# A transformer layer on one core: the score scale moved into queries and keys, maxima stored negated, and the weight maxima in another order

## What is computed

```python
q = (norm(x) @ Wqa @ Wqb)            # 16 heads x (64 plain + 64 rotary)
c_kv, k_pe = split(norm(x) @ Wkva)   # 64 latent + 64 rotary, shared by all heads
q_pe, k_pe = rope(q_pe), rope(k_pe)
scores = q_full @ k_full.T * 128 ** -0.5, causal
probs = softmax(scores)
attn = probs @ v ; x = x + attn @ Wo
x = x + top-2-of-16 experts(norm(x)) + shared expert(norm(x))
```

## Time and profile before

| | us |
|---|---|
| time before, median of 3 runs (1613.17 to 1618.74) | 1617.57 |
| the profiled execution, its own time | 1630.28 |
| its span, first to last instruction | 1627.2 |

### The profile page before, as it was taken

One profiled execution on the slowest core, in us unless ns is written; L12 is line 12 of the kernel. 1 busy time (PEld: TensorE's weight loads), 2 busy tenths in 40 slices (PEclk: granted clock), 3 DMA queues, 4 the chain that ended last, 5 costly groups with the idle time before them and its releaser, 6 DMA issues.

```text
span 1627.2 us, 45245 instructions
## 1 busy us (share of the span) xinstructions
PE 1500.0 (92%) x16430; PEld 1089.0 (67%) x16431; DVE 1290.8 (79%) x3107; ACT 1030.5 (63%) x2344; POOL 989.1 (61%) x1596
## 2 busy tenths in 40 slices
PE   9878999999889999998899999988999999889990
PEld 3355777777667777776667777766677777667870
DVE  2587888888878889888788888888787888766676
ACT  1366666666667666666566666665766666557770
POOL 3257774536288754656888777677886755264440
PEclk6799999999999999999999999999999999999995
DMA  6255753321363333203643322135543210347518
GB/s 189 37 120 134 165 83 63 65 58 35 63 123 70 75 65 70 58 17 72 110 92 70 70 61 54 29 73 95 104 67 63 58 34 16 103 123 242 162 56 314
DMA packets 331031, 144.69 MB, mean 89 GB/s; under 512 B 278498, under 2 KB 321541, under 8 KB 330824
## 3 DMA queue, kind: packets, MB, share of 16 engines
q1 hardware_dynamic: 305744, 105.67, 32.3%
q10 hardware_dynamic: 18168, 19.41, 4.0%
q0 software_dynamic: 6912, 16.83, 3.1%
HBM read 47.04 MB, written 29.53 MB: 47 GB/s over the span
## 4 chain that ended last, share of the span: by engine, by line
PE 64%; DVE 16%; ACT 5%; DMA 4%; issue 4%; SPq 1%; POOL 1%; ACTq 0%; DVEq 0%; POOLq 0%
PE of_ps L698 26%; PE s_ps L698 23%; PE t_ps L872 13%; DVE pT L1668 5%; DMA qT<-work 2%; DVE smax L1639 2%; DVE smax L1621 2%; ACT pT L1065 1%; ACT probs L1199 1%; PE of_ps L980 1%; PE t_ps L966 1%; ACT work L1065 1%; DVE weights L1878 1%; DVE o_sb L1502 1%; DVE smax L1643 1%
## 5 line engine op out<-in xcount | busy, mean ns | idle before, releaser
L1668 DVE TENSOR_TENSOR pT<-t_ps,pT 128x512 f16<-128x512 f32 (+3 forms) x688 | 409.7, 598 | 121.3 <-ACT pT L1065 118.4
L1065 ACT CAST pT<-t_ps 128x512 f16<-128x512 f32 (+3 forms) x688 | 354.6, 515 | 230.2 <-PE t_ps L872 229.0
L698 PE MATMUL s_ps<-kT,qT 128*128 128x512 f16 (+3 forms) x2112 | 474.9, 337 | 4.4 <-DMA qT<-work 3.7
L872 PE MATMUL t_ps<-id,probs 128*128 128x128 f32 x2304 | 381.0, 280 | 27.1 <-DVE pT L1668 15.9
L872 PEld LDWEIGHTS t_ps<-id,probs 128*128 128x128 f32 x2304 | 256.7, 142 | 123.1 <-issue 73.7
L1194 ACT ACTIVATE probs<-s_ps,nmax,fac 128x640 f32<-128x640 f32 (+3 forms) x256 | 269.1, 1051 | 0.2
L698 PEld LDWEIGHTS of_ps<-ckv,pT 128*128 128x128 f16 x6912 | 241.0, 98 | 41.8 <-DVE o_sb L1502 10.1
L698 PE MATMUL of_ps<-ckv,pT 128*128 128x64 f16 x6912 | 257.8, 193 | 7.7 <-DVE o_sb L1502 7.4
L698 PEld LDWEIGHTS s_ps<-kT,qT 128*128 128x128 f16 x2112 | 203.7, 98 | 71.6 <-DMA qT<-work 4.4
L698 PE MATMUL of_ps<-weights,xT 128*128 128x512 f16 (+1 forms) x936 | 197.9, 348 | 17.6 <-ACT work L1065 5.5
L1948 POOL TENSOR_TENSOR os_<-o_sb,os_ 128x512 f16<-128x512 f32 x60 | 70.1, 1169 | 153.3 <-ACT os_ L1065 151.4
(11 more groups left out here) (238 smaller groups left out, 2476.8 us busy)
## 6 DMA issues: line engine op xcount, KB each, us to landing
wgu_sb<-wgu ACTq DMA_DIRECT2D x8, 704.0 KB, 4.7
work<-lists SPq DMA_DIRECT2D x40, 128.5 KB, 2.3
qT<-lists SPq DMA_DIRECT2D x40, 128.5 KB, 2.8
x_sb<-x SPq DMA_DIRECT2D x32, 128.0 KB, 2.5
x<-x SPq DMA_DIRECT2D x32, 128.0 KB, 2.5
dense<-den SPq DMA_DIRECT2D x32, 128.0 KB
weights<-dense ACTq DMA_DIRECT2D x1, 4096.0 KB, 21.4
qT<-y_exp SPq DMA_DIRECT2D x16, 256.0 KB, 6.8
```

Source lines behind the costliest of these rows:

```text
L698: return pe_.matmul(o, a, b, start=start, stop=stop)
L872: last = pe_.transpose(t_ps[:, h, c * P:(c + 1) * P], probs[:, u % 2, g * L + j * P:g * L + (j + 1) * P], id32[:, :])
L1065: return act.copy(o, i)
L1668: dve.tensor_tensor(pT[:, u % 2, 1, h, 0:w], t_ps[:, h, 0:w], pT[:, u % 2, 0, h, 0:w], ALU.subtract).then_inc(s.lo_p, 1)
```

## The change

Four things are changed together.

1. `f_att` is split into two factors. `f_root` is about one over its square root, from the float's bits; keys are scaled by `f_k = 1 / f_root`, queries by `f_q = f_att * f_root`, as they are copied out of PSUM, and the output projection's factor takes `f_root` to undo the keys' part in `ckv`. Scores then come out of TensorE finished, and the exponentials need no scale.
2. Maxima are stored negated by the reduction itself, straight into `nmax`. The second instruction is gone, but for tile 7, where the smaller of the two negated halves is still to be found.
3. `SPLIT_MAX` picks halves for tiles 0 to 3 and 7; tile 6 goes by whole units now.
4. In `first_weights` the maxima of the query weights' blocks come as the blocks do, the other weights' maxima and the two `means` in between; `scales` is raised a first time before the new factors are made.

```diff
-SPLIT_MAX = [g > 1 or i >= 6 for i, g in enumerate(GROUP)]
+SPLIT_MAX = [g > 1 or i == 7 for i, g in enumerate(GROUP)]
...
+            def scaled(o, i, factor):
+                return act.activation(o, i, ACT.Copy, scale=factor)
...
-                copy(pe_of(n)[:, H, :], bank[:, C:2 * C])
-                copy(ks_sb[:, n % KS, 0, 0:C], bank[:, 0:C]).then_inc(s.hi_q, 1)
+                scaled(pe_of(n)[:, H, :], bank[:, C:2 * C], f_k)
+                scaled(ks_sb[:, n % KS, 0, 0:C], bank[:, 0:C], f_k).then_inc(s.hi_q, 1)
...
-                        act.activation(probs[:, par, 0:L], s_flat[:, 1024 * par:1024 * par + L], ACT.Exp, bias=nmax[:, par, 0:1],
-                                       scale=f_att, accum_out=ssum[:, t % 2, u:u + 1]).then_inc(s.exp_done, 2)
+                        act.activation(probs[:, par, 0:L], s_flat[:, 1024 * par:1024 * par + L], ACT.Exp, bias=nmax[:, par, 0:1],
+                                       accum_out=ssum[:, t % 2, u:u + 1]).then_inc(s.exp_done, 2)
...
+                dve.sem_inc(s.scales, 1)
                 link(dve.tensor_scalar(f_att, wamp[:, A_Q:A_Q + 1], wamp[:, A_KV:A_KV + 1], HD ** -0.5, ALU.mult, ALU.mult))
-                dve.tensor_scalar(f_natt, f_att, -1.0, None, ALU.mult)
+                link(dve.tensor_scalar(f_root.bitcast(I32), f_att.bitcast(I32), -0.5, SEED_K, ALU.mult, ALU.add))
+                dve.reciprocal(f_k, f_root)
+                link(dve.tensor_tensor(f_q, f_att, f_root, ALU.mult))
                 dve.sem_inc(s.scales, 1)
...
-                dve.tensor_tensor(ks_sb[:, n % KS, 1, 0:C], bank_of("lat", n)[:, 0:C], ks_sb[:, n % KS, 0, 0:C],
-                                  ALU.subtract).then_inc(released("lat", n)[0], 1)
+                dve.scalar_tensor_tensor(ks_sb[:, n % KS, 1, 0:C], bank_of("lat", n)[:, 0:C], f_k, ks_sb[:, n % KS, 0, 0:C],
+                                         ALU.mult, ALU.subtract).then_inc(released("lat", n)[0], 1)
...
-                dve.tensor_reduce(smax[:, par, 0:G], view, AX_X, ALU.max).then_inc(s.maxs, 1)
-                dve.wait_ge(s.maxs, g_ + 1)
...
+                most = dve.tensor_reduce(nmax[:, par, 0:G], view, AX_X, ALU.max, negate=True)
+                if not shifted(i, u):
+                    most.then_inc(s.max_ready, 1)
                     return
-                dve.tensor_scalar(nmax[:, par, 0:G], smax[:, par, 0:G], f_natt, None, ALU.mult).then_inc(s.max_ready, 1)
...
-                    last = dve.tensor_scalar(nmax[:, par, 0:1], smax[:, par, 0:1], smax[:, par, 1:2], f_natt, ALU.max, ALU.mult)
+                dve.tensor_tensor(nmax[:, par, 0:1], smax[:, par, 0:1], smax[:, par, 1:2], ALU.min).then_inc(s.max_ready, 1)
```

More of the change, by code:

```diff
@@ L128 @@
 SEED = 1597463007.0
+SEED_K = SEED - 3 * 2.0 ** 23
 A_Q, A_KV, A_O, A_SG, A_SD, A_R, A_GU, A_D = range(8)
@@ L1199, in exps @@
                     last = act.activation(probs[:, par, g * L:(g + 1) * L], s_flat[:, base:base + L],
-                                          ACT.Exp, bias=nmax[:, par, g:g + 1], scale=f_att,
+                                          ACT.Exp, bias=nmax[:, par, g:g + 1],
                                           accum_out=ssum[:, t % 2, u * G + g:u * G + g + 1])
@@ L1251, in section @@
                 side(t, units(t), 0)
+            act.wait_ge(s.scales, 2)
             latent_copies(0)
```

69 lines of the change are left out of this document (38 added, 31 removed).

## The result

| | before | after |
|---|---|---|
| median of the runs, us | 1617.16 (4 runs, 1613.17 to 1618.74) | 1592.43 (4 runs, 1587.21 to 1597.01) |
| the profiled execution, us | 1630.28 | 1597.01 |
| its span, us | 1627.2 | 1594.0 |

The ratio after to before is 0.9851, with an interval of 0.9827 to 0.9875: 24.7 us less, where the prediction had 14.2. Three later sets of runs, each with its own runs of the kernel before on the same chip, gave 0.9869 (0.9838 to 0.9900), 0.9879 (0.9865 to 0.9894) and 0.9875 (0.9843 to 0.9907), so the gain is nearer to 20 us.

A forecast was written before the change was run, and what follows sets the result against it. Attention was taken as bound by ScalarE and VectorE in the starts, and by TensorE, 46.98 of 49 us busy, in long tiles. -5.0 - 9.5 + 0.3 = -14.2 us off the 1617.6 median gave 1603; bounds 1597 to 1611, range 1596 to 1613.

The forecast's parts named there:

- The unit prices: Per instruction: 0.10 us for a ScalarE pointer, 0.06 for a VectorE one, 0.25 for a maximum's second instruction, negation nothing.
- rival B: Exponentials: the bias pointer keeps the price, so dropping the scale pointer gains nothing; 1607 us, chance 0.08.
- rival D: Tile 6: waiting for the second half of scores delays a rest in 64 units, costing 22 us; 1628 us, chance 0.04.
- The distances of the earlier trace: From one place of tile 4 to the same of tile 5: 2 us or more less in the second sequence, less in the third.
- The prologue: First weights: new order of maxima costs and gains nothing, the longer path to first scores counts +0.3 us; bounds -0.3 and +0.5.
- The long tiles: Whole maxima, tile 7 pairs and exponentials on the chain give 14.3 us, of which two thirds arrive: 9.5 us less.
- Tile 6: One reduction of 896 elements instead of two halves saves 0.15 to 0.35 us a unit, 0.25 taken; gain 2.3 us.
- rival C: Starts and long tiles: waits shrink by the full chain, all of 6.2 and 14.7 us; 1596 or a little less, chance 0.07.
- The starts: Starts of the four sequences: cheaper exponentials and rests less added factors give 6.2 us, four fifths taken: 5.0 us less.
- A: Long tiles: TensorE takes over at once, only 4.3 us and half of the start arrive; 1611 us, chance 0.17.
- E: Projection bank: 192 copies with a factor hold TensorE; the start loses 2, long tiles give 4.3; 1615 us, chance 0.08.
- Tile 7: A minimum of two tensors replaces a two-pointer multiplication of 0.27 us, saving 0.10 each; sign: minima under 0.2 us.

The follow-up runs named there:

- three pairs: Profiles, changed kernel against kernel before: the two profiled executions; both with the new order of first maxima; both with the old. Tiles 4 and 5: -9.7, -10.0, -7.8 us.
- set 1: Against the kernel before (1636.6 us): changed kernel again 1616.5, changed kernel with old order of first maxima 1620.6, before with new order alone 1633.0, before with 19 warm-ups 1636.6.

## Why the prediction was wrong

**What held.** The unit prices: 0.25 us for the second instruction (0.25 measured), nothing for the negation, 1.08 us for the reduction of 896 (1.089), 0.10 for a scale pointer on ScalarE (0.09, so rival B is out), 0.10 for a factor at a copy (585 to 687 ns for 512 columns, 232 to 316 for 64) and 0.06 for one at a rest (690 to 750 ns). VectorE's busy time fell by 65 us (75 said), ScalarE's by 24 (30 said). Each of the later sequences' starts is shorter by 0.8 to 1.3 us in the profiled pair (1 to 2 said), and tile 6 is not longer, so rival D is out. The distances of the earlier trace rows fell by 1.5 and 0.9 us, where 2 or more and less was said.

**The prologue.** This is the step that failed. It priced the new order at +0.3 us, as "the last block sets the end either way", with blocks every 4 us. That spacing was the low clock of this one execution. At the full clock blocks come every 2.1 us, VectorE's wait for POOL ahead of the last four (4.79 us) decides, and the new order takes it away: 5.4 us to the first rest (73.8 to 68.4) and about 4 at the end. The chance was there to see: the execution lay 13 us above its median, and the section on the profile before already gave a mean clock of 0.70 in the first 85 us. What the prediction feared here, POOL late for `rope(0)`, did not come: POOL still waits 3.75 us ahead of it after the change. Where the 1 to 2 us between the first rest and the end go is only suggested: from the first rest to tile 4 of the first sequence the three kernels with the old order took 116.9 to 118.8 us and the eleven profiles with the new one 116.1 to 121.8, mean 119.9.

**The long tiles.** The mechanism was right and its size was off in tiles 4 and 5: 6.2 us priced, 7.8 to 10.0 in the three pairs of profiles. The second instruction alone, put back, costs 10.3 there. Tile 6 is near its price (2.7 to 2.8 us against 2.3). The thirty whole maxima on the chain and the two thirds of them that should arrive gave too little; my reading is that a chain counts the places where the operation is last now, and not those where it is second by less than its price. The 14.7 of rival C is too much for all three pairs (8.5 to 13.0 us).

**The starts.** 5.0 us forecast. The other three sequences gave 3.0, 4.4 and 6.6 in the three pairs, against 4.3 priced, so this term is neither confirmed closely nor refuted. The factor at copies cost more than was counted (3.7 us in three sequences by its removal, where 3 were forecast for all four). The first sequence scatters by some 5 us between executions and shows nothing.

**The rest of the miss.** In set 1 the change without the new order (the changed kernel with the old order) is worth 16.0 us in the medians, where the prediction's other terms make 14.5; with the new order it is 20.1, against 14.2. So of the 5.9 us missed there 4.4 are the prologue (+0.3 counted, 4.1 less measured), and 1.5 the rest. The first comparison, of four runs each, shows 4.6 us more than set 1, which makes up the 10.6 us between 1603 and 1592.4. The three later ratios of 0.9869 to 0.9879 give 1596 to 1598 on the prediction's base, at the range's lower edge of 1596; why the first comparison lies beyond them is open, and may be scatter. Among the rivals C came nearest (1596), though by another sum, so its nearness is luck; A and E, which had the gains absorbed, are out.

**Tile 7.** "Under 0.2 us" held for 38 of the 64 minima. The mean was 0.307, since the new operation waits for POOL. The old multiplication did not: its 128 executions took 272 to 275 ns, beside POOL or not. Tile 7 was priced at 1.0 us less; it took 0.5 less in one pair and 0.6 and 2.0 more in the others.

## What to carry to other kernels

Before a sum is made against a profiled execution that lies above the median, find the stretch in which the difference lies and price the edits in that stretch for the usual execution too: a slow stretch hides waits. Beside a TensorE that is busy 96% of a stretch, a quarter of a microsecond taken off VectorE's path in each unit still arrived by a third to a half; measure that share in the tile in question, since here it was about 0.13 in one tile and 0.52 in the next. And of two operations with the same result take the one with a single SBUF input when POOL is at work: here it was 0.155 us against up to 1.26.

## What the runs showed of the hardware

- TensorE's granted clock was 0.50 (1.2 GHz) from 12 to 50 us in the profiled execution of before, though TensorE was busy without a gap from 8.8 us on, and 1.00 from 12 to 30 us in the profile after and in the four of set 1, with 15 or 19 warm-ups ahead. By the mean clock 3 of 47 executions of the kernel before and one with the new order were of that kind, 12 to 13 and 23 us longer.
- With the old order TensorE is idle for 5.55 us behind its last fold, and the granted clock is 0.50 from 34 to 44 us; with the new order it is 1.00 all through 30 to 50 us.
- A minimum of two [128, 1] tensors took 0.16 us on VectorE in most cases, and up to 1.26 us when it began while POOL was in a longer operation; a reduction over two neighbours took 0.154 to 0.156 us in all 192 cases, of which 79 lay inside an operation of POOL.
- A wait between two dependent VectorE operations cost 0.12 us of overlap on top of the second one's 0.13 (0.25 us in the medians of 64 units each).
- A scale pointer beside a bias pointer cost 0.09 us on ScalarE in eight sizes from 128 to 1024, and a reduction that negates took as long as a plain one (948 and 949 ns).
